# A four-layer decoder on one core: in the last layer's state-space stage, one output product changes sides of the differences, and the bank waits move up by one product

## The chip, the cores and the metric

The program runs on one core of a Trainium2 chip, as one launch. The metric is the device time in microseconds (us); the median of three runs of the kernel before is 1874.9 us (1874.17 to 1876.9). The core has a matmul engine (PE) with its own weight loads (PEld), a vector engine (DVE), an activation engine (ACT), a general engine (POOL) and a queue engine for transfers (SP). They run at the same time and wait for each other through semaphores. PE writes only to eight accumulation banks of 128 rows by 512 fp32 numbers, `ps[0]` to `ps[7]`.

## The reference

Four layers, each with a self-attention or state-space part, a cross-attention and a feed-forward part, on 8 x 128 tokens of width 256. The change lies in the last layer's state-space part, which for 64 heads of width 64 computes, per chunk of 128 tokens:

```python
zxbcdt = hidden_states @ W_in                     # z and x of every head, B, C, dt
xbc = _causal_conv1d(xbc, conv_w, conv_b)         # four taps, then silu
dA_cs = jnp.cumsum(dt * A, axis=chunk)
diff = dA_cs[:, :, :, None] - dA_cs[:, :, None, :]
L = jnp.exp(jnp.where(mask, diff, -jnp.inf))      # lower triangle alone
Y = jnp.einsum('bcign,bcjgn,bcijgh,bcjghp->bcighp', Cm, Bm, L, dtx)
y = y + D * x
yg = y * _silu(z)
out = (yg * rms(yg) * norm_w) @ W_out
```

With one chunk for each of the 8 blocks of tokens there is no state that is carried on.

## The kernel before

The stage `l3_attn` runs as 32 passes, one for each pair of heads. Passes 0 to 3 are written out; passes 4 to 31 are a loop of 14 turns with two passes in each, an even one (slot 0) and an odd one (slot 1). Every engine has its own program for a pass, and the order on an engine is the order in which the code is written; no planner moves anything. The stretch between the odd pass and the next even one holds the loop's branch.

For pass j, PE does this (functions `pair`, `output`, `differences`, `make_y`):

- **Output products**, L2797: the gated result of pass j - 3 times its slice of the output matrix. Eight products, one for each block of 128 tokens, add into banks 0 to 3. A product is a 128 x 128 by 128 x 256 fp32 matmul and stands in the trace as two loads and two matmuls.
- **Bank waits**, `free_for_differences` at L2747 to L2756: the differences write banks 4 to 7, which DVE reads as x transposed (`xt_read`, set by L3080) and as y (`y_read`, set by L3045). PE waits for both readers and for POOL's `steps_ready`.
- **Differences**: 16 small matmuls on 32 x 32 tiles lay the mask down (mask tiles, L2764), then four matmuls of 512 columns (L2769) add the differences of the running sums, one bank each, with `diff_psum`.
- **x and z products**, L2827: 12 matmuls for x into banks 4 and 5, 12 for z into banks 6 and 7, each bank after ACT has read its difference (`diff_read`).
- **y**, L2784: 32 matmul records, in two halves, for pass j - 1, into banks 6 and 7, after ACT has read z (`z_read`, L2950).
- **Transposes of x**, L2839, in two halves, each after ACT's silu of x (`x_ready`, L2952), into banks 4 and 5.

ACT in a pass: four exponents of the differences (L2913), the squares of a gated result (L2920), the first tap of the convolution for each half of x (L2658, after `x_psum`), a table load (L2944), silu of z (L2950) and silu of x (L2952) in turns, a table load (L2955). DVE: four multiplications of the exponents with the masked C-B product (L3032), three more taps for each half (L2662), the skip term on y (L3045), dt times x from the transposes (L3080), the gate (L3054). POOL adds squares (L3129), prepares the rows for the differences (L3122, L3124), splits weights in high and low parts (L3147, L3150), and scales the next slice of the output matrix (L3136) after `out_done`, which the eighth output product sets; after that it lets SP load the next weights (`slot_read`).

Of the kernel before, what the change touches and what calls it, by code (L numbers as in the profile page):

```python
# [2584 lines left out]
def l3_attn(k):  # L2585
# [11 lines left out]
    with Stage(k, "L3a", k.now) as st:  # L2597
# [55 lines left out]
        def bank(name, n):  # L2653
            return ps[BANK[name] + n]
# [18 lines left out]
        def is_first(j):  # L2673
            return isinstance(j, int) and j == 0

        def is_second(j):
            return isinstance(j, int) and j == 1

        def early(j, n=2):

            return isinstance(j, int) and j < n

        ln = Norm(k, st)
        with nc.Block() as block:
# [14 lines left out]
            def _(pe):  # L2699
# [15 lines left out]
                def make_cs(pe):  # L2715

                    pe.wait_ge(S["zdt"], 1)
                    pe.wait_ge(S["dA_rows"], 1)
                    pe.wait_ge(S["dA_rows_act"], 1)
                    for dp in range(ND):  # L2720
                        mm = nc.tensor.matmul(ps[dp // 4][:, (dp % 4) * P:(dp % 4 + 1) * P], dax[:, dp, :], triu,
                                              start=True, stop=True)
                        if dp % 4 == 3:
                            mm.then_inc(S["cs_psum"], 1)

                def make_cb(pe):

                    pe.wait_ge(S["bc_ready"], 2)
                    for b in range(NB):
                        if b % 4 == 0:  # L2730
                            pe.wait_ge(S["cs_high"], b // 4 + 1)
                        mm = nc.tensor.matmul(ps[b // 4][:, (b % 4) * P:(b % 4 + 1) * P], bT[:, b * P:(b + 1) * P],
                                              cT[:, b * P:(b + 1) * P], start=True, stop=True)
                        if b % 4 == 3:
                            mm.then_inc(S["cb_psum"], 1)

                def clear_sums(pe):

                    pe.wait_ge(S["cb_ready"], 2)
                    pe.wait_ge(S["cs_high"], 4)  # L2740
                    pe.wait_ge(S["zero_set"], 2)
                    for n in range(4):
                        nc.tensor.matmul(ps[n][:, :], zero[:, :], xnT[:, 0, 0:HALF], start=True, stop=False,
                                         skip_group_check=True)

                def free_for_differences(pe, j, i):
                    pe.wait_ge(S["steps_ready"], i + 1)  # L2747
                    for n in range(4):
                        if is_first(j):
                            pe.wait_ge(S["xt_read" if n < 2 else "z_read"], n % 2 + 1)  # L2750
                        elif is_second(j):
                            pe.wait_ge(S["diff_read"], n + 1)
                        elif n < 2:
                            pe.wait_ge(S["xt_read"], j * 2 - 1 + n)
                        else:
                            pe.wait_ge(S["y_read"], j * 2 - 5 + n)  # L2756

                def differences(pe, s):

                    for turn in range(4):  # L2760
                        for n in range(4):
                            g, own = (n + turn) % 4, slice(32 * n, 32 * n + 32)
                            out = bank("d", n)[32 * g:32 * g + 32, :].rearrange("p (b t) -> p b t", b=4)
                            nc.tensor.matmul(out[:, :, 0:32 * g + 32], ident32[own, :],  # L2764
                                             over(later[own, g, 0:32 * g + 32], 4), start=True, stop=False,
                                             skip_group_check=True)
                    for n in range(4):
                        g = slice(32 * n, 32 * n + 32)
                        nc.tensor.matmul(bank("d", n)[:, :], lrow[g, s, :], rrow[g, :, :].rearrange("p m t -> p (m t)"),  # L2769
                                         start=False, stop=True, skip_group_check=True).then_inc(S["diff_psum"], 1)  # L2770
# [18 lines left out]
                def output(pe, j, o, half, part=range(4), of_next=None):  # L2789

                    pe.wait_ge(S["wo_ready"], j + 1)
                    pe.wait_ge(S["y_ready"], j * 2 + half + 1)
                    for b in part:
                        g = 4 * half + b
                        if b == part[-1] and of_next is not None:
                            free_for_differences(pe, *of_next)
                        mm = nc.tensor.matmul(ps[g // 2][:, (g % 2) * C:(g % 2 + 1) * C],  # L2797
                                              yg[:, o, g * P:(g + 1) * P], wo[:, o, :], start=False, stop=False,
                                              skip_group_check=True)
                    if half == 1 and part[-1] == 3:  # L2800
                        mm.then_inc(S["out_done"], 1)

                def pair(pe, j, s, i):
                    first = is_first(j)
                    if is_second(j):
                        clear_sums(pe)
                    if not early(j, 3):
                        output(pe, j - 3, 1 - s, 0)
                        output(pe, j - 3, 1 - s, 1, (0, 1), (j, i))
                    elif not first:  # L2810
                        free_for_differences(pe, j, i)
                    if not first:
                        differences(pe, s)
                    if not early(j, 3):
                        output(pe, j - 3, 1 - s, 1, (2, 3))
                    if first:
                        make_cs(pe)
                    pe.wait_ge(S["w_split"], j + 1)
                    for at_d, (name, wm, sem) in enumerate((("x", wx[s], "x_psum"), ("z", wz[s], "z_psum"))):
                        for half in range(2):  # L2820
                            if first:
                                pe.wait_ge(S["bc_conv"], at_d + 1)
                            else:
                                pe.wait_ge(S["diff_read"], j * 4 + 2 * at_d + half + 1)
                            for kc in range(KC):
                                for at, (a, b) in enumerate(THREE):
                                    mm = nc.tensor.matmul(bank(name, half)[:, :], wm[a][:, kc, :],  # L2827
                                                          (xh, xl)[b][:, kc, half * HALF:(half + 1) * HALF],
                                                          start=(kc + at == 0), stop=(kc + at == KC + 1))
                            mm.then_inc(S[sem], 1)  # L2830
                    if first:
                        make_cb(pe)
                    else:
                        make_y(pe, j, 1 - s)
                    for half in range(2):
                        pe.wait_ge(S["x_ready"], j * 2 + half + 1)
                        for b in range(4):
                            g = 4 * half + b
                            mm = nc.tensor.transpose(bank("t", half)[:, b * P:(b + 1) * P],  # L2839
                                                     xT[:, s, g * P:(g + 1) * P], k.ident)  # L2840
                        mm.then_inc(S["xt_psum"], 1)
                    if first:
                        free_for_differences(pe, j, i)
                        differences(pe, s)
# [16 lines left out]
                pe.wait_ge(S["x_low"], 1)  # L2861
                pe.wait_ge(S["mask_set"], 2)
                passes(pe, pair, tail)

            @block.scalar
# [1056 lines left out]
```

## Time and profile before

| what | value |
|---|---|
| median of three runs | 1874.9 us (1874.17 to 1876.9) |
| the profiled execution's own time | 1872.17 us |
| its span, first to last instruction | 1870.0 us |
| PE busy | 1655.7 us (89%) |
| DVE busy | 1175.1 us (63%) |
| ACT busy | 931.7 us (50%) |
| POOL busy | 461.8 us (25%) |
| mean granted TensorE clock | 0.955 |
| the 32 passes of this stage, with output products | about 1129 to 1535 us of the span |

The shares are means over all stages, which have different limits, so the stage has to be read by itself. PE's matmuls are pipelined: the records of neighbouring matmuls overlap, and a PE that is busy is not a PE at its peak. The PEld rows (weight loads) show better where PE stands still. A row's end is its start plus its duration, and where a row groups several instructions the duration runs from the start of the first to the end of the last.

### The profile page before, as it was taken

To read this page: it belongs to the slowest core of one execution; us is meant where nothing else is said; L and a number is where in the kernel's file an instruction comes from. 1 tells how busy PE (TensorE), PEld (TensorE's weight loads), DVE (VectorE), ACT (ScalarE), POOL (GpSimd) and SP (SyncE) were. 2 spreads that over 40 slices of the span, in tenths; PEclk is the share of its full clock that TensorE was granted. 3 is DMA by queue.
4 is the path that set the end of the run, shared out by engine and by line. 5 is a ranking of instruction groups with operands and counts; after the bars stand their busy time and mean duration, and the time that the engine had idled before them with its cause. 6 is when DMAs were issued, how large, how long until landed. Compare 5 with 4: busy or idle time off the path is not lost. (4 is left out here: it accounts for less than half of the span.)

```text
span 1870.0 us, 38238 instructions
## 1 busy us (share of the span) xinstructions
PE 1655.7 (89%) x14220; PEld 1276.5 (68%) x14220; DVE 1175.1 (63%) x2316; ACT 931.7 (50%) x1979; POOL 461.8 (25%) x510
## 2 busy tenths in 40 slices
PE   7988856789999889996688869999999987999898
PEld 4767733558888745663477747777777766888687
DVE  4676688556666622224665588888888875666642
ACT  2455567236656521121255456676766644555552
POOL 2030021023333131221400225454454531000220
PEclk9999978799999999998799889999999998999999
DMA  2020000300000092222000100010101003111000
GB/s 103 3 94 3 4 30 31 117 18 27 26 25 25 18 371 45 47 35 67 14 2 3 50 18 27 26 34 26 34 26 33 27 9 126 35 34 34 1 1 24
DMA packets 27684, 77.91 MB, mean 42 GB/s; under 512 B 2993, under 2 KB 14897, under 8 KB 25393
## 3 DMA queue, kind: packets, MB, share of 16 engines
q1 hardware_dynamic: 23488, 71.19, 11.1%
q0 software_dynamic: 4080, 5.13, 1.7%
q8 instruction: 79, 1.29, 0.3%
q14 instruction: 37, 0.30, 0.1%
HBM read 63.03 MB, written 13.28 MB: 41 GB/s over the span
## 5 line engine op out<-in xcount | busy, mean ns | idle before, releaser
L2662 DVE SCALAR_TENSOR_TENSOR arena<-bank,arena 128x508 f32<-128x508 f32 (+2 forms) x204 | 151.5, 743 | 18.4 <-DVE arena L2662 6.6
L3032 DVE TENSOR_TENSOR L3a_decays<-L3a_decays,L3a_cb_masked 128x512 f32<-128x512 f32 x128 | 94.8, 799 | 49.5 <-ACT L3a_decays L2913 49.5
L2797 PE MATMUL bank<-L3a_wo,L3a_y_gated 128*128 128x256 f32 x512 | 125.0, 388 | 0.0
L2913 ACT ACTIVATE L3a_decays<-bank 128x512 f32<-128x512 f32 x128 | 66.1, 604 | 103.3 <-PE bank L2769 103.3
L2827 PE MATMUL bank<-L3a_xnT_high,L3a_w_high 128*128 128x512 f32 x256 | 105.1, 410 | 1.5 <-ACT L3a_decays L2913 1.5
L2797 PEld LDWEIGHTS bank<-L3a_wo,L3a_y_gated 128*128 128x128 f32 x512 | 91.2, 190 | 21.0 <-issue 11.4
L228 PE MATMUL bank<-const 128*128 128x512 f32 (+1 forms) x154 | 73.7, 619 | 33.7 <-PEq L66 33.7
L2827 PE MATMUL bank<-L3a_xnT_high,L3a_w_low 128*128 128x512 f32 x256 | 100.5, 392 | 0.0
L2827 PE MATMUL bank<-L3a_xnT_low,L3a_w_high 128*128 128x512 f32 x256 | 100.2, 391 | 0.0
L3129 POOL TENSOR_TENSOR arena<-arena 128x1024 f32<-128x1024 f32 x32 | 86.3, 2695 | 44.4 <-ACT arena L2920 44.4
L2064 ACT ACTIVATE arena<-bank 128x512 f32<-128x512 f32 x23 | 13.7, 597 | 145.4 <-PE bank L2013 145.4
L2013 PE MATMUL bank<-L1f_experts,xnT 128*128 x184 | 85.0, 606 | 0.8 <-DVE xnT L2116 0.6
L228 PEld LDWEIGHTS bank<-const 128*128 128x128 f32 x154 | 29.2, 201 | 65.6 <-issue 65.4
L827 ACT ACTIVATE L1x_p<-bank,L1x_minus_max,L1x_q_scale 128x128 f32<-128x128 f32 x128 | 56.6, 452 | 32.0 <-DVE L1x_minus_max L1861 32.0
L2784 PE MATMUL bank<-L3a_decays,L3a_dtx 128*64 128x128 f32 x1024 | 67.2, 279 | 3.9 <-ACT arena L2950 2.1
L2784 PEld LDWEIGHTS bank<-L3a_decays,L3a_dtx 128*64 128x64 f32 x1024 | 54.8, 136 | 22.0 <-ACT arena L2950 17.9
L827 ACT ACTIVATE L3x_p<-L3x_masked_scores,L3x_minus_max 128x128 f32<-128x128 f32 x128 | 49.7, 389 | 38.8 <-DVE L3x_minus_max L3368 38.8
L2110 DVE TENSOR_TENSOR L1f_hidden<-arena,bank 128x512 f32<-128x512 f32 x23 | 15.8, 688 | 82.5 <-PE bank L2013 82.5
L1974 POOL DMA_INDIRECT rows_added<-L1f_y,L1f_token x23 | 35.7, 1554 | 114.9 <-DVE L1f_y L2129 111.8
L1689 POOL TENSOR_TENSOR L1x_q_squares<-L1x_qT 128x512 f32<-128x512 f32 x32 | 36.6, 1161 | 101.6 <-ACT L1x_qT L1802 101.6
L672 POOL TENSOR_TENSOR x<-x,arena 128x256 f32<-128x256 f32 x48 | 34.6, 756 | 109.3 <-ACT xn L215 96.4
L2952 ACT ACTIVATE L3a_xT<-arena 128x512 f32<-128x512 f32 x64 | 40.2, 628 | 37.8 <-DVEq L3070 37.8
(643 smaller groups left out, 4654.5 us busy)
## 6 DMA issues: line engine op xcount, KB each, us to landing
arena<-in_L3p SPq DMA_DIRECT2D x32, 388.0 KB, 3.0
L1f_experts<-in_L1f SPq DMA_DIRECT2D x8, 1536.0 KB, 18.9
arena<-in_L1x SPq DMA_DIRECT2D x18, 384.0 KB, 3.0
arena<-in_L3x SPq DMA_DIRECT2D x18, 384.0 KB, 3.0
arena<-in_L0f SPq DMA_DIRECT2D x1, 4224.0 KB, 12.9
arena<-in_L3f SPq DMA_DIRECT2D x1, 4055.0 KB, 12.8
rows_sent<-L1a_blank SPq DMA_DIRECT2D x1, 2967.0 KB, 13.6
xnT<-rows_sent SPq DMA_DIRECT2D x23, 129.0 KB, 2.0
```

The lines of the kernel that those rows point to most:

```text
L228: self.nc.tensor.matmul(self.k.ps[bank][:, 0:width], self.k.ident, self.k.const[:, 0:width], start=True, stop=True)
L827: ins = nc.scalar.activation(self.p[:, h, b * P:(b + 1) * P], src[:, b * P:(b + 1) * P], ACT.Exp, bias=self.nb[:, h, b:b + 1], scale=scale ...
L1689: nc.gpsimd.tensor_tensor(sq[:, h * HALF:(h + 1) * HALF], q, q, ALU.mult).then_inc(s_sq, 1)
L2013: mm = nc.tensor.matmul(ps[2 * (t % 2) + m][:, :], rowsT[:, t % 2, kc, :], experts[:, bass.ds(first + (m * KC + kc) * I, I)], start=(kc == 0),
L2662: return nc.vector.scalar_tensor_tensor(dst[:, :, d:], psum[:, :, 0:P - d], wcol, dst[:, :, d:], ALU.mult, ALU.add)
L2784: mm = nc.tensor.matmul(bank("y", half)[h * HD:(h + 1) * HD, b * P:(b + 1) * P], dtx[:, o, g, h, :], dec[:, o, h, g, :], start=True, stop= ...
L2797: mm = nc.tensor.matmul(ps[g // 2][:, (g % 2) * C:(g % 2 + 1) * C], yg[:, o, g * P:(g + 1) * P], wo[:, o, :], start=False, stop=False, ski ...
L2827: mm = nc.tensor.matmul(bank(name, half)[:, :], wm[a][:, kc, :], (xh, xl)[b][:, kc, half * HALF:(half + 1) * HALF], start=(kc + at == 0), ...
L2913: nc.scalar.activation(d4[:, n * HALF:(n + 1) * HALF], bank("d", n)[:, :], ACT.Exp).then_inc(S["diff_read"], 1)
L2952: nc.scalar.activation(xT[:, s, t], conv[:, s, 4 * half:4 * half + 4, :].rearrange("p b t -> p (b t)"), ACT.Silu).then_inc(S["x_ready"], 1)
L3032: nc.vector.tensor_tensor(d, d, cbm[:, 4 * half:4 * half + 4, :].rearrange("p b t -> p (b t)"), ALU.mult).then_inc(S["dec_ready"], 1)
L3129: nc.gpsimd.tensor_tensor(sqsum, sqsum, ysq, ALU.add).then_inc(S["sq_added"], 1)
```

## The change

The third argument group of `output` names which of the four products of a half are issued, and the last argument asks for the bank waits before the last product named. Before, products 1 to 6 stood ahead of the differences, with the bank waits ahead of the sixth, and products 7 and 8 behind. Now products 1 to 5 stand ahead, with the bank waits ahead of the fifth, and products 6 to 8 behind. This holds for passes 3 to 31; passes 0 to 2 have no output products.

```diff
                     if not early(j, 3):
                         output(pe, j - 3, 1 - s, 0)
-                        output(pe, j - 3, 1 - s, 1, (0, 1), (j, i))
+                        output(pe, j - 3, 1 - s, 1, (0,), (j, i))
                     elif not first:
                         free_for_differences(pe, j, i)
                     if not first:
                         differences(pe, s)
                     if not early(j, 3):
-                        output(pe, j - 3, 1 - s, 1, (2, 3))
+                        output(pe, j - 3, 1 - s, 1, (1, 2, 3))
```

On PE in the odd pass of the loop, before the change; L2754 and L2756 are the bank waits, a row without a count is one product or one instruction, and the last row is the first of the mask tiles:

```order
L2792 ISA
L2797 MATMUL bank<-L3a_wo,L3a_y_gated 128x256 x4
L2792 REGISTER_ALU
L2797 MATMUL bank<-L3a_wo,L3a_y_gated 128x256
L2754 ISA
L2756 REGISTER_ALU x2
L2797 MATMUL bank<-L3a_wo,L3a_y_gated 128x256
L2764 MATMUL bank<-L3a_later_tiles,L3a_ident 32x4x32
```

The same place after the change:

```order
L2792 ISA
L2797 MATMUL bank<-L3a_wo,L3a_y_gated 128x256 x4
L2792 REGISTER_ALU
L2754 ISA
L2756 REGISTER_ALU x2
L2797 MATMUL bank<-L3a_wo,L3a_y_gated 128x256
L2764 MATMUL bank<-L3a_later_tiles,L3a_ident 32x4x32
```

The product that stood between the fourth and the waits is gone from here; one product still stands between the waits and the mask tiles.

Behind the differences of the same pass, on PE, one piece of the difference between the two programs (L2818 and L2824 are registers and a wait of the x products):

```order
 L2764 MATMUL bank<-L3a_later_tiles,L3a_ident 32x4x96
 L2769 MATMUL bank<-L3a_diff_right,L3a_diff_left 128x512 x4
-L2797 MATMUL bank<-L3a_wo,L3a_y_gated 128x256 x2
+L2797 MATMUL bank<-L3a_wo,L3a_y_gated 128x256 x3
 L2818 REGISTER_ALU
 L2824 ISA
```

Three products now stand between the differences and the x products. The other engines have the same instructions in the same order.

## Rows read from the trace of the kernel before

**Rows 1.** Busy us (instructions) in a stretch: PE PEld DVE ACT POOL, clock, DMA.
```profile
1128.00:1520.00 392.00, 386.24 (x2895) 294.05 (x2891) 322.99 (x463) 268.22 (x377) 192.09 (x199) 1.00 0.10 29
```

**Rows 2.** Waits, 1128 to 1520 us: waiter <- releaser: total us, times, longest.
```profile
ACT L3a_decays L2913 <- PE bank L2769: 87.1, 29, 3.2
DVE L3a_decays L3032 <- ACT L3a_decays L2913: 42.8, 29, 1.8
POOL arena L3129 <- ACT arena L2920: 37.5, 29, 1.3
DVE arena L2662 <- ACT arena L2658: 4.7, 29, 0.2
```

**Rows 3.** Timeline, outputs to differences, even pass: start, us, engine, line [idle before].
```profile
1294.62 0.14 PEld L2764 LDWEIGHTS bank<-L3a_later_tiles,L3a_ident 32*32 32x32 bf16 x16 [0.33 <-issue]
...
1305.48 2.46 PEld L2797 LDWEIGHTS bank<-L3a_wo,L3a_y_gated 128*128 128x128 f32 x12 [0.16 <-issue]
1305.79 1.28 DVE L3080 TENSOR_TENSOR L3a_dtx<-bank,L3a_dt_pair 128x512 f32<-128x512 f32 x2
1307.10 0.84 PEld L2797 LDWEIGHTS bank<-L3a_wo,L3a_y_gated 128*128 128x128 f32 x4
1308.27 0.14 PEld L2764 LDWEIGHTS bank<-L3a_later_tiles,L3a_ident 32*32 32x32 bf16 x16 [0.33 <-issue]
```

**Rows 4.** Timeline, the same place in the next, odd pass.
```profile
1319.52 1.28 DVE L3080 TENSOR_TENSOR L3a_dtx<-bank,L3a_dt_pair 128x512 f32<-128x512 f32 x2
1320.57 0.41 PEld L2797 LDWEIGHTS bank<-L3a_wo,L3a_y_gated 128*128 128x128 f32 x2
1321.12 0.30 PEld L2797 LDWEIGHTS bank<-L3a_wo,L3a_y_gated 128*128 128x128 f32 x2 [0.15 <-issue]
1321.75 0.14 PEld L2764 LDWEIGHTS bank<-L3a_later_tiles,L3a_ident 32*32 32x32 bf16 x16 [0.33 <-issue]
```

**Rows 5.** Timeline between those two places: from the differences to dt times x.
```profile
1309.05 1.13 PE L2797 MATMUL bank<-L3a_wo,L3a_y_gated 128*128 128x256 f32 x4
1309.23 2.07 ACT L2913 ACTIVATE L3a_decays<-bank 128x512 f32<-128x512 f32 x4 [3.08 <-PE bank L2769]
1309.86 2.92 DVE L3032 TENSOR_TENSOR L3a_decays<-L3a_decays,L3a_cb_masked 128x512 f32<-128x512 f32 x4 [1.58 <-ACT L3a_decays L2913]
...
1310.25 0.40 PE L2827 MATMUL bank<-L3a_xnT_low,L3a_w_high 128*128 128x512 f32 x1
...
1311.17 0.39 PE L2827 MATMUL bank<-L3a_xnT_high,L3a_w_low 128*128 128x512 f32 x1
1312.11 0.80 ACT L2658 ACTIVATE arena<-bank,arena 128x512 f32<-128x512 f32 x1
1312.53 0.39 PE L2827 MATMUL bank<-L3a_xnT_high,L3a_w_low 128*128 128x512 f32 x1
1312.94 2.30 DVE L2662 SCALAR_TENSOR_TENSOR arena<-bank,arena 128x508 f32<-128x508 f32 x3 [0.16 <-ACT arena L2658]
1312.96 0.79 ACT L2658 ACTIVATE arena<-bank,arena 128x512 f32<-128x512 f32 x1
...
1315.48 2.30 DVE L2662 SCALAR_TENSOR_TENSOR arena<-bank,arena 128x508 f32<-128x508 f32 x3 [0.24 <-DVE arena L2662]
...
1317.73 0.42 PEld L2839 LDWEIGHTS bank<-const,L3a_xT 128*128 128x128 f32 x4 [0.17 <-issue]
1317.87 0.63 ACT L2952 ACTIVATE L3a_xT<-arena 128x512 f32<-128x512 f32 x1 [1.21 <-DVEq L3070]
1318.19 1.41 DVE L3045 SCALAR_TENSOR_TENSOR L3a_y_gated<-L3a_xT,L3a_d_pair,bank 128x512 f32<-128x512 f32 x2 [0.41 <-PE bank L2784]
...
1318.55 0.42 PEld L2839 LDWEIGHTS bank<-const,L3a_xT 128*128 128x128 f32 x4 [0.40 <-ACT L3a_xT L2952]
```

**Rows 6.** Timeline, pass 3, the last that is written out.
```profile
1129.43 1.28 DVE L3080 TENSOR_TENSOR L3a_dtx<-bank,L3a_dt_pair 128x512 f32<-128x512 f32 x2
...
1132.20 0.14 PEld L2764 LDWEIGHTS bank<-L3a_later_tiles,L3a_ident 32*32 32x32 bf16 x16 [0.33 <-issue]
```

## The prediction

> **What bounds the kernel now.** I began with the stage alone, since the change touches nothing else. PE is busy 386.24 of 392 us there at a granted clock of 1.00, the upper of its two levels (2.4 GHz), and nobody else is above 323 [rows 1]. Read alone, that says that PE is the bound and that the order of its products can't matter: it issues the same instructions before and after. But matmul records overlap, so I went on to the waits. ACT stands 87.1 us in 29 passes for the differences, 3.0 us each; DVE stands 42.8 us for ACT's exponents, 1.5 us each [rows 2]. The question is whether those waits lie on a circle that sets the length of a pass.
>
> I followed one pass through the timeline. From the mask tiles at 1308.27 [rows 3]: ACT's first exponent starts at 1309.23, DVE's multiplications at 1309.86 and run to 1312.78, ACT (exponents, squares, first tap) lets DVE's taps start at 1312.94, the second half of them ends at 1317.78, DVE's skip term runs from 1318.19 to 1319.60 [rows 5], its dt times x from 1319.52 to 1320.80, and the next mask tiles start at 1321.75 [rows 4]. From the multiplications on DVE hardly pauses: 0.16 and 0.24 us around the taps, 0.41 ahead of the skip term. So the circle is: differences, ACT's first exponent, DVE through to dt times x (with ACT's first tap just in time), bank wait, differences. 1321.75 - 1308.27 = 13.48 us, of which 12.53 us run from the mask tiles to the end of L3080, and 0.95 us from there to the next mask tiles. PE is not the bound; it pauses inside the pass, for 0.40 us ahead of the second transposes for one [rows 5].
>
> **The release, in the two kinds of passes.** Call R the end of L3080, from which the banks are free. In the odd pass R is 1319.52 + 1.28 = 1320.80. The fifth product's loads start at 1320.57 and end at 1320.98; the sixth's start at 1321.12 after 0.15 us of standing, where the usual step is 0.03; the mask tiles follow at 1321.75 [rows 4]. So the sixth product was held by the bank waits: it starts at R + 0.32, and the mask tiles at R + 0.95. In the even pass R is 1305.79 + 1.28 = 1307.07. The fifth product starts at 1307.10, its four loads and those of the sixth run without a gap (0.84 us for four), so a load takes a step of (0.84 - 0.19) / 3 = 0.217 us and a product 0.43 us; the mask tiles start at 1308.27, which is R + 1.20 [rows 3]. There nothing waited: the sixth product came at PE's own pace, since PE starts its outputs late there, with the loop's branch between (0.16 us of issue ahead of them). (0.19 us is the duration of a single load, as the pair of 0.41 us shows: 0.41 - 0.217.)
>
> **What the change takes away, ahead of the differences.** One product, 0.43 us, leaves the path, but the waits move with it and still stand ahead of a product. What follows a release is the same string as before: waits, one product, mask tiles, which the odd pass shows to be 0.95 us.
> - Odd passes: the fifth product could start at 1320.57 by PE's pace, but is held until R + 0.32 = 1321.12, where the sixth is now. The mask tiles stay at R + 0.95. Gain 0. What the product gave back turns into standing, 0.55 us.
> - Even passes: the fifth could start at 1307.10, is held until R + 0.32 = 1307.39, and the mask tiles come at R + 0.95 = 1308.02. Gain 1.20 - 0.95 = 0.25 us. The loop has 14 even passes; the first of them (pass 4) does not come behind the branch, and I leave it out: 13 x 0.25 = 3.2 us.
> - Pass 3: R is 1130.71, the mask tiles 1132.20, R + 1.49 [rows 6]. PE's pace rules; a product less is 0.43, and the string of 0.95 would allow 0.54. Gain 0.4.
>
> The sum is 3.2 + 0.4 = 3.6 us. The bounds of the string behind the release are these rows: 0.95 (as the odd pass) and 1.20 (as the even pass, nothing gained but pass 3's 0.4); I take the first, since the held product there has just the neighbours that it will have.
>
> **What it adds, behind the differences.** In 29 passes the x and z products start one product, 0.43 us, later after their differences. Today they start without standing: the last product's matmul ends at 1309.05 + 1.13 = 1310.18 and the second x matmul at 1310.25 + 0.40 = 1310.65, two steps of 0.235, where x matmuls in a stream take steps of (1312.53 - 1311.17) / 6 = 0.227 [rows 5]; the wait for the first exponent is just covered. So nothing of the 0.43 is paid back there, and what lies beside it has to be found row by row, all in [rows 5]:
> - ACT's first tap, first half, needs the sixth x matmul: 1311.17 + 0.39 = 1311.56, and starts at 1312.11, when ACT has done the squares. Cover 0.55, less 0.04 us that the second half shows from matmul to ACT (1312.92 to 1312.96): 0.51 against 0.43. It holds by 0.08.
> - The second half is held by PE already (1312.96) and will be 0.43 later, 1313.39 to 1314.18; DVE needs it at 1315.48. Cover 1.3 us. Everything of ACT behind it (table load, both silus of z, the first of x) moves too, up to the second silu of x at 1317.87, ahead of which ACT stood 1.21 us.
> - y on PE moves by 0.43, and so do the first transposes: 1318.16 instead of 1317.73, ending some 0.4 later. The second transposes wait for ACT until 1318.55 after a pause of 0.40. They come 0 to 0.05 later; DVE needs them only for the second L3080.
> - The eighth product sets `out_done` 0.43 later for POOL's L3136. Queued behind it are the release of the weights' slot to SP and the sum of squares L3129, which stands 1.3 us for ACT in each pass [rows 2]. Cover 1.3 against 0.43; the transfer that SP then starts serves the next pass but one, as before.
>
> So the added 0.43 costs nothing on the circle, though one of its covers is thin.
>
> The Trainium skill speaks against the change here. The rows show twelve loads in 2.46 us, one each 0.217, beside matmuls that go on [rows 3, 5]. By "TensorE: Matmul & The Clock Gate", Part 3, The mechanism, a weight load overlaps with matmuls in flight only when its row group differs; all output products use all 128 rows, so load and matmul would follow each other. The trace disagrees with that sentence, and agrees with the same page's statement that loads are pulled ahead.
>
> **How the times stand.** The profiled execution took 1872.17 us for a span of 1870.0; less 3.6 that is 1868.6. The median of the runs is 2.7 us above the profiled one, so the same change gives 1874.9 - 3.6 = 1871.3 us.
>
> **The rivals.**
> - *The waits do not bind, and every pass gains a product.* 29 x 0.43 = 12.5 us, 1862.4 us. For it: ACT's wait of 3.0 us in all 29 passes [rows 2], and differences that do come one product earlier in the program. Against it: the sixth product already stands for the release in the odd pass [rows 4].
> - *The string behind the release is longer with the waits at the fifth.* If it takes 1.20 instead of 0.95 in the even pass, as the branch pass has other register work, only pass 3 gains: 1874.5 us. For it: only odd passes show the 0.95. Against it: the same waits and the same product follow.
> - *Slower: the third product holds up ACT's first tap.* The second half of it is already released by PE to within 0.04 us, and DVE stands for the first half in all 29 passes (4.7 us, [rows 2]). If the 0.51 of cover is not there, since squares could start earlier or x products come later than I put them, the taps, L3080 and the next differences come up to 0.43 later in each of the 28 passes that follow: 28 x 0.43 = 12.0, less 3.6, is 8.4 us slower, 1883.3 us. It decides as soon as x arrives more than 0.08 us later than I reckon, and makes the whole slower than before from 0.13 us a pass on (3.6 / 28).
> - *Loads do not overlap.* A product behind the differences would then cost two loads of 0.19 us and two matmuls of at least their step of 0.22, 0.82 us in all, 0.31 beyond the cover: 28 x 0.31 = 8.7, less 3.6, 1880.0 us. Twelve loads in 2.46 us speak against it [rows 3]. That is what the Trainium skill's sentence above would give.
>
> That the change doesn't do what it says is out: PE's order of instructions shows it.
>
> **Numbers.** Forecast 0.70, with a range of its own of 1869.5 to 1873.5; all passes gain 0.06; only pass 3 gains 0.12; slower by the first tap 0.11; loads do not overlap 0.01. The measurement tells about 0.2% (3.75 us) from no change, so faster means below 1871.15. The forecast lies 0.15 us short of that; I give half of it to each side: faster 0.35 + 0.06 = 0.41, same 0.35 + 0.12 = 0.47, slower 0.12. The range goes from just under the forecast's own to the case of pass 3 alone with the spread of the runs: 1868.5 to 1876; it leaves out 0.06 and 0.12.
>
> **What would show it.** In the profile after: mask tiles at R + 0.95 in even and odd passes alike, where before they came at 1.20 and 0.95; a standing of about 0.3 us in even and 0.55 us in odd passes ahead of the fifth product's loads; two passes together 26.9 us instead of 27.13 (1321.75 - 1294.62, odd pass to odd pass, [rows 3, 4]); ACT's wait for the differences shorter by 0.25 in every second pass only; DVE's wait for ACT ahead of the taps still 0.16; the pause ahead of the second transposes gone. The prediction is wrong if the first tap starts later than 3.85 us after the mask tiles (slower), or if odd passes become shorter (the release itself has moved).

## The result and the profile after

The changed kernel took 1869.28 us (median of 14 runs, 1864.77 to 1874.99), the kernel before 1875.0 in the same comparison (14 runs, 1873.16 to 1879.55). The ratio is 0.9967, 95% interval 0.9955 to 0.9979: 6.2 us faster (3.9 to 8.4); the ratio takes in every run, and the two medians lie 5.7 us apart. The forecast was 3.6 us faster, 1871.3. The profiled execution's span is 1862.7 us, 7.3 below before.

First the place on which the sum rested. The timeline after, from the outputs to the mask tiles in an even pass (start, us, engine, line; idle before in brackets):

```profile
1300.11 1.59 PEld L2797 LDWEIGHTS bank<-L3a_wo,L3a_y_gated 128*128 128x128 f32 x8
1300.43 1.28 DVE L3080 TENSOR_TENSOR L3a_dtx<-bank,L3a_dt_pair 128x512 f32<-128x512 f32 x2
1302.03 0.30 PEld L2797 LDWEIGHTS bank<-L3a_wo,L3a_y_gated 128*128 128x128 f32 x2 [0.33 <-issue]
1302.66 0.14 PEld L2764 LDWEIGHTS bank<-L3a_later_tiles,L3a_ident 32*32 32x32 bf16 x16 [0.33 <-issue]
```

R is 1300.43 + 1.28 = 1301.71, the fifth product's loads start at R + 0.32 after standing 0.33 us, and the mask tiles at R + 0.95, where they came at R + 1.20 before [rows 3]. The next, odd pass, with the mask tiles of the odd pass before it in the first row:

```profile
1289.25 0.14 PEld L2764 LDWEIGHTS bank<-L3a_later_tiles,L3a_ident 32*32 32x32 bf16 x16 [0.33 <-issue]
...
1313.41 1.60 PEld L2797 LDWEIGHTS bank<-L3a_wo,L3a_y_gated 128*128 128x128 f32 x8
1313.91 1.28 DVE L3080 TENSOR_TENSOR L3a_dtx<-bank,L3a_dt_pair 128x512 f32<-128x512 f32 x2
...
1315.52 0.30 PEld L2797 LDWEIGHTS bank<-L3a_wo,L3a_y_gated 128*128 128x128 f32 x2 [0.51 <-issue]
1316.15 0.14 PEld L2764 LDWEIGHTS bank<-L3a_later_tiles,L3a_ident 32*32 32x32 bf16 x16 [0.33 <-issue]
```

R is 1315.19; loads at R + 0.33 after 0.51 us of standing, mask tiles at R + 0.96, as before [rows 4]. Odd passes gained nothing. Two passes take 1316.15 - 1289.25 = 26.90 us, where they took 27.13.

Then the covers: how long each engine could be kept waiting before the circle would feel it. The timeline of the stretch between:

```profile
1303.45 1.16 PEld L2797 LDWEIGHTS bank<-L3a_wo,L3a_y_gated 128*128 128x128 f32 x6 [0.24 <-issue]
...
1306.50 0.80 ACT L2658 ACTIVATE arena<-bank,arena 128x512 f32<-128x512 f32 x1
1307.34 2.30 DVE L2662 SCALAR_TENSOR_TENSOR arena<-bank,arena 128x508 f32<-128x508 f32 x3 [0.17 <-ACT arena L2658]
1307.81 0.78 ACT L2658 ACTIVATE arena<-bank,arena 128x512 f32<-128x512 f32 x1 [0.51 <-PE bank L2827]
...
1312.27 0.63 ACT L2952 ACTIVATE L3a_xT<-arena 128x512 f32<-128x512 f32 x1 [0.76 <-DVEq L3070]
...
1312.58 0.86 PEld L2839 LDWEIGHTS bank<-const,L3a_xT 128*128 128x128 f32 x8 [0.17 <-issue]
```

The first row is the three products behind the differences. The first tap starts 3.84 us after the mask tiles (1306.50 - 1302.66), exactly as before, so the thin cover held. Its second half now stands 0.51 us for PE; ACT's pause ahead of the second silu of x shrank from 1.21 to 0.76, and PE's pause ahead of the second transposes is gone: all eight loads run in one row, where they stood in two with 0.40 between [rows 5]. The waits of the stage in total (1125 to 1513 us; those of before are in [rows 2]):

```profile
ACT L3a_decays L2913 <- PE bank L2769: 83.4, 29, 3.0
DVE L3a_decays L3032 <- ACT L3a_decays L2913: 39.2, 29, 1.4
...
POOL arena L3129 <- ACT arena L2920: 20.1, 29, 0.7
...
ACT arena L2658 <- PE bank L2827: 14.6, 29, 0.5
```

ACT's and DVE's waits on the circle fell by 3.7 and 3.6 us, as much as the stage became shorter. They are two links of one circle, so the two numbers are the same 3.6 us seen twice. POOL used 17 us of its cover (0.6 a pass, of 1.3), and ACT's wait for x is new and costs nothing.

**Where 7.3 us come from.** The mask tiles of pass 2 are the last place ahead of any changed instruction; those of pass 31 are the last in the loop. (The table of the profile before has the 32 passes from about 1129 us; that is where the first output products stand, and the mask tiles of pass 0 already come at 1096.4.) Before, at those two places:

```profile
1117.66 0.17 PEld L2764 LDWEIGHTS bank<-L3a_later_tiles,L3a_ident 32*32 32x32 bf16 x16 [1.81 <-issue]
...
1511.82 0.14 PEld L2764 LDWEIGHTS bank<-L3a_later_tiles,L3a_ident 32*32 32x32 bf16 x16 [0.33 <-issue]
```

After, at the same two, with those of pass 3 between:

```profile
1113.86 0.17 PEld L2764 LDWEIGHTS bank<-L3a_later_tiles,L3a_ident 32*32 32x32 bf16 x16 [1.81 <-issue]
...
1127.94 0.14 PEld L2764 LDWEIGHTS bank<-L3a_later_tiles,L3a_ident 32*32 32x32 bf16 x16 [0.33 <-issue]
...
1504.55 0.14 PEld L2764 LDWEIGHTS bank<-L3a_later_tiles,L3a_ident 32*32 32x32 bf16 x16 [0.33 <-issue]
```

The stretch took 394.16 us and takes 390.69: 3.5 us, against 3.6 reckoned. Of these, pass 3 is 14.54 - 14.08 = 0.46 (its mask tiles of before stand in [rows 6]) and the loop 3.0. The other 3.8 us were there at pass 2, in code that is the same in both; behind pass 31 both take 358.2 us to the end. Ten microseconds of layer 1's first stage show where most of it is, busy us by engine (instructions), then the granted clock; before:

```profile
368.00:378.00 10.00, 10.00 (x30) 5.98 (x30) 6.30 (x22) 1.51 (x6) 0.00 (x0) 0.66 0.00 1
```

and after:

```profile
368.00:378.00 10.00, 10.00 (x46) 6.48 (x44) 9.33 (x31) 2.13 (x8) 0.00 (x0) 1.00 0.00 1
```

In both executions PE had stood 8.2 us for DVE shortly before, and the granted clock of 357 to 368 us is 0.53. In the execution after, the clock was back at its upper level (2.4 GHz) some 7 us earlier, and PE issued 46 matmuls instead of 30. The same two pairs of matmuls, before:

```profile
365.62 1.33 PE L1515 MATMUL bank<-L1a_spec,const 128*128 128x288 f32 x2
...
375.10 0.75 PE L1515 MATMUL bank<-L1a_spec,const 128*128 128x288 f32 x2
```

and after:

```profile
364.98 1.33 PE L1515 MATMUL bank<-L1a_spec,const 128*128 128x288 f32 x2
...
371.33 0.75 PE L1515 MATMUL bank<-L1a_spec,const 128*128 128x288 f32 x2
```

The first pair comes 0.64 us earlier and the second 3.77, so 3.1 of the 3.8 us arise between them, with the clock. Whether that belongs to the program or to the one execution was the open question after the result.

### The profile page after: what moved, and what is told of

It reads as the page before. It is cut to its first block and busy times, and to the rows that moved or that the text cites. A ratio compares the mean times of both kernels' runs of the same rounds, so it can differ in the third digit from the quotient of the medians.

```text
span 1862.7 us, 38248 instructions
## 1 busy us (share of the span) xinstructions
PE 1647.6 (88%) x14216; PEld 1275.9 (68%) x14220; DVE 1175.1 (63%) x2316; ACT 932.2 (50%) x1979; POOL 467.5 (25%) x510
## 3 DMA queue, kind: packets, MB, share of 16 engines
q1 hardware_dynamic: 23488, 71.19, 11.1%
## 5 line engine op out<-in xcount | busy, mean ns | idle before, releaser
L2797 PE MATMUL bank<-L3a_wo,L3a_y_gated 128*128 128x256 f32 x512 | 130.9, 393 | 1.7 <-issue 0.3
L3136 POOL TENSOR_TENSOR L3a_wo<-arena 128x256 f32<-128x256 f32 x32 | 28.9, 903 | 133.0 <-PE bank L2797 133.0
```

## The experiments

Each diff is against the kernel that it starts from: the one before where its first line has `(0, 1)`, else the changed one. Stage times below are from the mask tiles of pass 2 to those of pass 31, in one profile each: 394.16 us before, 390.69 in the changed kernel. Line numbers of the fences shift by up to two where an edit adds or takes lines.

**The changed kernel once more.** The same code.

> The changed kernel once more, for the part of the difference that the changed stage does not show (its profile was 7.3 us below that of before, of which 3.8 us were there before the stage began, where both programs are the same). If that is the granted clock of the matmul engine rising at another moment in that one execution: the stage from the mask tiles of pass 2 to those of pass 31 again 3.5 us shorter than before (390.7 instead of 394.2), the part ahead of the stage again different by some us, to either side, and a ratio nearer 0.998. If the surplus belongs to the program: again 3.8 us less ahead of the stage and a ratio of 0.9967.

Measured: 1869.78 us (12 runs) against 1872.96 of the kernel before (25 runs), ratio 0.9981, interval 0.9968 to 0.9995: 3.6 us faster (0.9 to 6.0). The profile of this second execution:

```profile
1118.34 0.17 PEld L2764 LDWEIGHTS bank<-L3a_later_tiles,L3a_ident 32*32 32x32 bf16 x16 [1.82 <-issue]
...
1133.59 0.14 PEld L2764 LDWEIGHTS bank<-L3a_later_tiles,L3a_ident 32*32 32x32 bf16 x16 [0.33 <-issue]
...
1510.02 0.14 PEld L2764 LDWEIGHTS bank<-L3a_later_tiles,L3a_ident 32*32 32x32 bf16 x16 [0.33 <-issue]
```

Pass 2 is reached at 1118.34, 0.7 us later than before, not 3.8 earlier. The loop from pass 3 on takes 376.43 us, in the first profile of the changed kernel 376.61, before 379.62. The stage as a whole is 391.7 and not 390.7, since pass 3 took 15.25 us instead of 14.08; the granted clock was 0.78 over that pass and 0.88 in the first profile (and before). Where pass 3 ran at another clock, the loop alone is the better measure. With pass 2 reached later and the loop as short as in the first profile, the surplus ahead of the stage belongs to the execution. All nine profiles of this case reach pass 2, by code that is the same up to the output products, between 1113.86 and 1119.44 us, and the first one of the changed kernel is the lowest of them. The second ratio lies on the forecast; the first interval's near end (3.9 us) just misses the 3.5 us that the stage shows. The changed kernel's medians are nearly the same in the two comparisons (1869.28 and 1869.78); it is the kernel before that came out at 1875.0 in one, 1872.96 in the other and 1876.02 in a third.

**The waits alone.** Six products ahead as before, the waits at the fifth:

```diff
-                        output(pe, j - 3, 1 - s, 1, (0, 1), (j, i))
+                        output(pe, j - 3, 1 - s, 1, (0,), (j, i))
+                        output(pe, j - 3, 1 - s, 1, (1,))
```

> One part of the change alone: the bank waits move up to the fifth product, but six products stay ahead of the differences. Release theory (what follows the end of dt times x, R, is a fixed string: waits, then every product behind them, then the mask tiles): mask tiles at R + 0.95 + 0.43 = R + 1.38 us in every pass; against before that is 0.43 later in 14 odd passes and 0.19 later in 14 even ones, 8.7 us slower than the kernel before (ratio 1.005). Rival (the products ahead of the differences count, wherever the waits stand): same products ahead, so the same time as before, ratio 1.000.

Measured: ratio 1.0043 (1.0025 to 1.0062), 8.0 us slower; stage 404.2 us, 10.0 more than before. Of these 1.1 lie in pass 3, where the granted clock was 0.78 against 0.88; the loop is 8.9 us longer, against 8.7 reckoned. The timeline of an odd pass:

```profile
1326.61 1.28 DVE L3081 TENSOR_TENSOR L3a_dtx<-bank,L3a_dt_pair 128x512 f32<-128x512 f32 x2
1328.22 0.73 PEld L2797 LDWEIGHTS bank<-L3a_wo,L3a_y_gated 128*128 128x128 f32 x4 [0.59 <-issue]
1329.28 0.14 PEld L2764 LDWEIGHTS bank<-L3a_later_tiles,L3a_ident 32*32 32x32 bf16 x16 [0.33 <-issue]
```

R is 1327.89, the held product at R + 0.33, the mask tiles at R + 1.39; even passes show the same string. What follows the release is a string of fixed length, and the second product in it costs its 0.43 us (R + 1.38 in both kinds of passes, against 0.95). The rival, by which only the number of products ahead counts, is out.

**The odd passes alone.**

```diff
-                        output(pe, j - 3, 1 - s, 1, (0, 1), (j, i))
+                        output(pe, j - 3, 1 - s, 1, (0,) if s else (0, 1), (j, i))
...
-                        output(pe, j - 3, 1 - s, 1, (2, 3))
+                        output(pe, j - 3, 1 - s, 1, (1, 2, 3) if s else (2, 3))
```

> The change in odd passes alone (pass 3 and the 14 odd ones of the loop); even passes keep six products ahead and the waits at the sixth. Release theory: odd passes gain nothing, since the sixth product was held by the release already, and pass 3 gains 0.4: 0.4 us faster than before, ratio 1.000; mask tiles at R + 0.95 in odd passes and still R + 1.19 in even ones. Rival (each moved product gives its share): half of the whole change, ratio 0.998 to 0.999, with odd passes shorter than 13.48 us.

Measured: ratio 0.9991 (0.9981 to 1.0000), stage 394.25 us, 0.1 more than before; the two kinds of passes take 13.66 (even) and 13.49 us (odd, median), before 13.65 and 13.48. The ratio by itself would allow the rival; the passes don't: odd ones are as long as before, so they gain nothing from the moved product. Pass 3's gain of 0.45 is there in the profile and is given back behind it: 0.33 in pass 4, which took 13.29 before and takes 13.62, and the rest in small differences of the others.

**Four products ahead.** One step further in the same direction, the waits at the fourth, four products behind.

```diff
-                        output(pe, j - 3, 1 - s, 0)
-                        output(pe, j - 3, 1 - s, 1, (0,), (j, i))
+                        output(pe, j - 3, 1 - s, 0, range(4), (j, i))
...
-                        output(pe, j - 3, 1 - s, 1, (1, 2, 3))
+                        output(pe, j - 3, 1 - s, 1)
```

> One step further: four products ahead of the differences, the waits at the fourth, four products behind. Release theory with the cover worked out in the prediction (first tap on ACT has 0.51 us of cover, a product costs 0.43): mask tiles stay at R + 0.95; the x products come 0.86 us later than before, which is 0.35 beyond the cover, so the first tap starts at 4.19 us after the mask tiles instead of 3.84 and every pass grows by 0.35: about 10 us slower than the changed kernel, some 6 us slower than before (ratio 1.003). Rival (the product behind the differences is free, as ACT stands 3 us for them): the same time as the changed kernel, ratio 0.997 or 0.998.

Measured: ratio 1.0035 (1.0021 to 1.0050), 6.6 us slower than before, with the stage at 401.14 us, 10.5 more than in the changed kernel (0.9 of it in pass 3, where the granted clock was 0.77 against 0.88; 9.6 in the loop). The timeline:

```profile
1296.94 0.14 PEld L2764 LDWEIGHTS bank<-L3a_later_tiles,L3a_ident 32*32 32x32 bf16 x16 [0.33 <-issue]
...
1301.13 0.78 ACT L2658 ACTIVATE arena<-bank,arena 128x512 f32<-128x512 f32 x1 [0.22 <-PE bank L2826]
1301.95 2.30 DVE L2662 SCALAR_TENSOR_TENSOR arena<-bank,arena 128x508 f32<-128x508 f32 x3 [0.50 <-ACT arena L2658]
...
1308.45 1.28 DVE L3079 TENSOR_TENSOR L3a_dtx<-bank,L3a_dt_pair 128x512 f32<-128x512 f32 x2
...
1310.68 0.14 PEld L2764 LDWEIGHTS bank<-L3a_later_tiles,L3a_ident 32*32 32x32 bf16 x16 [0.33 <-issue]
```

The first tap starts at 4.19 us after the mask tiles, as reckoned, now held by PE; DVE's pause ahead of the taps grew from 0.17 to 0.50; from the release, R = 1309.73, the mask tiles still take 0.95. That is the slower rival of the prediction, real one product further on. A third product behind the differences is free, a fourth costs 0.34 us a pass (9.6 / 28; reckoned 0.35).

**The waits behind the fifth product.** The mask tiles stand directly behind the waits; the last wait ends in an increment of a semaphore `banks_free` that nobody reads. Its entry in the list of semaphores is left out of this diff and of the next two.

```diff
                         output(pe, j - 3, 1 - s, 0)
-                        output(pe, j - 3, 1 - s, 1, (0,), (j, i))
+                        output(pe, j - 3, 1 - s, 1, (0,))
+                        free_for_differences(pe, j, i)
+                        pe.sem_inc(S["banks_free"], 1)
```

> The changed kernel, with the bank waits behind the fifth product instead of ahead of it (they end in an increment of a semaphore that nobody reads, directly ahead of the mask tiles). Release theory: the fifth product runs at PE's own pace and only 0.32 us remain from R to the mask tiles, so PE's pace rules: mask tiles at about 13.05 us after the last ones in odd passes (13.49 in the changed kernel) and 13.25 in even ones (13.42), 0.6 us in two passes, 8.5 us in 14 turns: 12 us faster than before, ratio 0.9935. Rival (DVE alone sets the circle, PE's string is hidden): same time as the changed kernel.

Measured: 1861.69 us (6 runs) against 1872.96, ratio 0.9944 (0.9925 to 0.9963), 10.5 us faster than before by the ratio (the medians lie 11.3 apart); stage 382.65 us, 11.5 less than before and 8.0 less than the changed kernel. The timeline, an even and an odd pass:

```profile
1299.53 2.02 PEld L2797 LDWEIGHTS bank<-L3a_wo,L3a_y_gated 128*128 128x128 f32 x10
1299.85 1.28 DVE L3082 TENSOR_TENSOR L3a_dtx<-bank,L3a_dt_pair 128x512 f32<-128x512 f32 x2
1301.88 0.14 PEld L2764 LDWEIGHTS bank<-L3a_later_tiles,L3a_ident 32*32 32x32 bf16 x16 [0.33 <-issue]
...
1312.62 2.03 PEld L2797 LDWEIGHTS bank<-L3a_wo,L3a_y_gated 128*128 128x128 f32 x10
1313.14 1.28 DVE L3082 TENSOR_TENSOR L3a_dtx<-bank,L3a_dt_pair 128x512 f32<-128x512 f32 x2
1314.98 0.14 PEld L2764 LDWEIGHTS bank<-L3a_later_tiles,L3a_ident 32*32 32x32 bf16 x16 [0.33 <-issue]
```

The ten loads of the five products run without a gap, and the mask tiles follow at R + 0.75 and R + 0.56: now PE's pace rules. By the medians (R + 0.76 and R + 0.57, before R + 1.19 and R + 0.95) these are 0.43 us in thirteen even passes and 0.38 in fourteen odd ones, 10.9 us, and pass 4 gives 0.15; the loop gave 11.0. The rival, by which DVE alone sets the circle, is out. This is the fastest kernel of the case.

**The waits behind the sixth product.** The same, with the order of the kernel before:

```diff
-                        output(pe, j - 3, 1 - s, 1, (0, 1), (j, i))
+                        output(pe, j - 3, 1 - s, 1, (0, 1))
+                        free_for_differences(pe, j, i)
+                        pe.sem_inc(S["banks_free"], 1)
```

> The order of the kernel before, six products ahead of the differences, but the bank waits behind the sixth. Release theory: PE's own pace then rules in both kinds of passes; in even ones it did before (R + 1.19), in odd ones the mask tiles move from R + 0.95 to about R + 0.93: 0.3 us in all, ratio 1.000. Rival (the gain of the waits behind the fifth, 11 us, comes from the place of the waits alone): ratio 0.995.

Measured: ratio 0.9991 (0.9979 to 1.0003), stage 393.95 us, 0.2 less than before; mask tiles at R + 1.19 in even passes and R + 0.93 in odd ones. An odd pass:

```profile
1319.54 1.28 DVE L3082 TENSOR_TENSOR L3a_dtx<-bank,L3a_dt_pair 128x512 f32<-128x512 f32 x2
...
1321.75 0.14 PEld L2764 LDWEIGHTS bank<-L3a_later_tiles,L3a_ident 32*32 32x32 bf16 x16 [0.33 <-issue]
```

The rival's 0.995 is out, and with it the added increment as a cause. The gain of 11 us needs both moves: with six products PE's pace rules anyway, with the waits ahead of the fifth the release does.

**The waits behind the fourth product.**

```diff
                         output(pe, j - 3, 1 - s, 0)
-                        output(pe, j - 3, 1 - s, 1, (0,), (j, i))
+                        free_for_differences(pe, j, i)
+                        pe.sem_inc(S["banks_free"], 1)
...
-                        output(pe, j - 3, 1 - s, 1, (1, 2, 3))
+                        output(pe, j - 3, 1 - s, 1)
```

> Four products ahead of the differences, the bank waits behind the fourth, four products behind the differences. Release theory: mask tiles at R + 0.33, which is 0.43 earlier than with the waits behind the fifth in even passes (0.76) and 0.24 earlier in odd ones (0.57); but the first tap comes at 4.21 after the mask tiles instead of 3.84, as in the kernel with four products ahead, 0.35 later in both. Even passes 13.14 us (13.22), odd 13.21 (13.11): the same as with the waits behind the fifth within 0.5 us, ratio 0.994 to 0.995. Rival (earlier differences win every time): 10 us less again, ratio 0.989.

Measured: ratio 0.9949 (0.9935 to 0.9963), stage 386.72 us, 4.1 more than with the waits behind the fifth, where I expected the same within 0.5. The ratio lies where it was expected and can't tell the two kernels apart (0.9944 and 0.9949); the 4.1 us stand in one profile each. The rival (0.989) is out; my numbers were short in two places. The timeline of two passes:

```profile
1318.26 0.17 PEld L2764 LDWEIGHTS bank<-L3a_later_tiles,L3a_ident 32*32 32x32 bf16 x16 [0.53 <-issue]
...
1322.48 0.78 ACT L2658 ACTIVATE arena<-bank,arena 128x512 f32<-128x512 f32 x1 [0.21 <-PE bank L2828]
...
1329.81 1.28 DVE L3081 TENSOR_TENSOR L3a_dtx<-bank,L3a_dt_pair 128x512 f32<-128x512 f32 x2
1331.49 0.31 PEld L2764 LDWEIGHTS bank<-L3a_later_tiles,L3a_ident 32*32 32x32 bf16 x16 [0.41 <-issue]
...
1335.86 0.78 ACT L2658 ACTIVATE arena<-bank,arena 128x512 f32<-128x512 f32 x1 [0.22 <-PE bank L2828]
```

R is 1331.09, the mask tiles come at R + 0.40 and not 0.33, and in this even pass their sixteen loads take 0.31 us instead of 0.14, after which the first tap comes at 4.37 instead of 4.21. In the odd pass ahead of it the loads take 0.17, though PE had stood longer there, and the tap comes at 4.22. The loads of the even pass, in two parts:

```profile
1331.49 0.13 PEld L2764 LDWEIGHTS bank<-L3a_later_tiles,L3a_ident 32*32 32x32 bf16 x6 [0.41 <-issue]
...
1331.68 0.12 PEld L2764 LDWEIGHTS bank<-L3a_later_tiles,L3a_ident 32*32 32x32 bf16 x10
```

The sixteen are not slow one by one: they come close together but for one stop ahead of the seventh. In twelve of the fourteen even passes the sixteen take 0.25 us or more, in the odd ones of the loop always 0.17. So the places of the loss are shown, 0.08 us behind R in the passes of the loop and the stop in even ones; what PE waits for at the stop is not. A held wait directly ahead does not explain it alone, since the odd passes have that too.

## Why the prediction was right, step by step

- **The circle and the release.** Right. From the mask tiles to R it was 12.46 us (to an even pass) and 12.53 (to an odd one) before, and stays 12.47 and 12.54 in the changed kernel (medians; 12.27 and 12.33 for pass 4). The waits alone and the waits behind the fifth move the loop by the string behind R: 8.9 us against 8.7 reckoned, and 11.0 against 11.1.
- **Odd passes 0, even passes 0.25, pass 3 0.4.** Measured: odd 0, even 0.23 (period 13.65 to 13.42, medians), pass 4 0.01, pass 3 0.46; in all 3.5 against 3.6. One reading beside the sum was off: twelve loads in 2.46 us are steps of (2.46 - 0.19) / 11 = 0.206 us on the mean and not 0.217, which holds for the last four alone. In [rows 3] the row of four loads is the end of the row of twelve.
- **The added product behind the differences costs nothing, with 0.08 us to spare at the first tap.** Right: the tap stayed at 3.84. That the spare was truly that thin was shown by the kernel with a fourth product, which lost 0.34 us a pass.
- **The standing ahead of the fifth product**, forecast 0.3 and 0.55, was 0.33 and 0.51.
- **The Trainium skill's sentence on weight loads.** Behind the differences six loads of three products now take 1.16 us (1303.45 to 1304.61 in the fence above), five steps of (1.16 - 0.19) / 5 = 0.19 us, while their matmuls run. The Trainium skill ("TensorE: Matmul & The Clock Gate", Part 3, The mechanism) has a sentence by which they would wait for matmuls of the same row group; neither this run nor any other here shows that. The same section of the Trainium skill also lets a load into the background weight buffer be pulled ahead, which the prediction did not weigh; these rows agree with it, and do not show the buffer itself.
- **The size.** The first comparison measured 6.2 us, nearly twice the forecast, the second 3.6. The 1869.28 us lie inside the stated range (1868.5 to 1876) and 0.2 below the forecast's own (1869.5 to 1873.5), so the mechanism was right and the whole time no better than near; that the second comparison fell on 3.6 exactly, with an interval of 0.9 to 6.0, is luck. No term of the sum was mis-sized in the stage; what was left out is that the rest of the program moves by some us from one execution to the next. That this carried the first comparison of 14 runs beyond what the stage gave is likely and not shown. What is still open is whether a small part of the first ratio is more than that: between its near end and the stage's 3.5 us there is 0.4 us.

## What to carry to other kernels

A wait holds everything written behind it: where the release comes last, ask what stands between it and the next step of the circle, and take that out (in the stage, five products with the waits behind the fifth gained 11.5 us, five with the waits still ahead of the fifth 3.5, and six with the waits behind the sixth 0.2, since PE's own pace ruled there). When work is moved off the circle, work out the cover of the engine that is first to need what it delays: here 0.51 us, enough for one product of 0.43 and not for two. And before a ratio is explained, compare the two traces up to the first changed instruction: half of the profile's difference was there already.

## What the runs showed of the hardware

- The granted clock of the matmul engine returned to its upper level at different moments of the same code from one execution to another: in layer 1's first stage 0.66 against 1.00 over the same 10 us, worth 3.1 us. Between the earliest and the latest arrival at pass 2 in nine profiles lie 5.6 us; how much of these is the clock was worked out for one pair of profiles only.
- From the end of dt times x to the load of the next product lie 0.32 to 0.33 us when PE stands at the bank waits (medians of odd and even passes, all kernels with the waits directly ahead of a product that they hold). In the changed kernel's even pass above, the trace has the record of the first wait instruction (L2754) 0.04 us after R, those of the next two (L2756) 0.11 and 0.09 further on, and the load 0.08 behind the last.
- Sixteen small weight loads take 0.14 us when a product stands ahead of them. In the kernel where they follow a held wait directly they take 0.17 in the loop's odd passes and, in twelve of its fourteen even ones, 0.25 to 0.31, with one stop ahead of the seventh load; the cause of the stop is not shown.
